# Layer 6: half 1's unrouted down products, the gate transposes and the bias products are issued behind the last routed tile

## What is computed

```python
xf = x.reshape(b * t, d)                     # 1024 tokens x 128
logits = xf @ Wg                             # 16 experts
_, topi = jax.lax.top_k(logits, 2)
gates = softmax(where(mask, logits, -inf))
y = 0
for e in range(16):                          # each token has 2 experts with a gate above 0
    h = silu(xf @ W1[e] + b1[e]) * (xf @ W11[e] + b11[e])        # 256 wide
    y = y + (h @ W2[e] + b2[e]) * gates[:, e, None]
z = silu(xf @ Ws1 + bs1) * (xf @ Ws11 + bs11) @ Ws2 + bs2        # 512 wide, every token
x = layernorm(x + y + z)
```

## Time and profile before

| | us |
|---|---|
| median of 3 runs | 660.75 |
| lowest, highest | 657.47, 665.46 |
| the profiled execution, its own time | 664.0 |
| its span in the profile | 662.2 |

### The profile page before, as it was taken

How to read it: one execution, slowest core, us unless ns; L and a number is a source line. 1 busy time by engine, 2 the same in 40 slices (tenths; PEclk the granted TensorE clock), 3 DMA queues, 4 the chain that set the end, 5 groups by cost and what they waited for, 6 DMA issues and landing times. The chain is left out here.

```text
span 662.2 us, 11995 instructions
## 1 busy us (share of the span) xinstructions
PE 469.6 (71%) x4136; PEld 363.4 (55%) x4136; DVE 442.6 (67%) x1480; ACT 266.9 (40%) x657; POOL 226.6 (34%) x265
## 2 busy tenths in 40 slices
PE   3788126583599768997858578968598895988850
PEld 2366113463577447775735457755377552687740
DVE  4899578979564776655583889974767572145535
ACT  5699511110013434653014637642375121165521
POOL 4131921636532002645010522310563136025540
PEclk9999657585799877997997768988899988899975
DMA  8100033100000040750000000000725001500112
GB/s 277 48 3 2 0 126 129 35 0 1 0 1 1 0 125 1 153 106 1 1 0 1 0 1 2 2 0 2 314 122 132 2 13 55 132 22 33 38 43 89
DMA packets 27966, 33.38 MB, mean 50 GB/s; under 512 B 4945, under 2 KB 21057, under 8 KB 27394
## 3 DMA queue, kind: packets, MB, share of 16 engines
q1 hardware_dynamic: 25970, 29.13, 14.9%
q0 software_dynamic: 1504, 3.15, 1.4%
q10 hardware_dynamic: 432, 0.33, 0.2%
HBM read 26.44 MB, written 6.16 MB: 49 GB/s over the span
## 5 line engine op out<-in xcount | busy, mean ns | idle before, releaser
L1789 POOL TENSOR_TENSOR ea_scaled_rows<-ea_scaled_rows 128x768 f32<-128x768 f32 (+2 forms) x24 | 27.8, 1156 | 62.0 <-ACT ea_scaled_rows L1716 60.8
L3210 POOL DMA_INDIRECT em_results<-em_y_slot,slot_rows x31 | 29.8, 960 | 51.5 <-DVE em_y_slot L3341 42.6
L3097 PE MATMUL banks<-em_slotT,em_weights 128*128 128x128 f32 x248 | 34.5, 283 | 4.2 <-ACT em_weights L2972 3.8
L219 ACT ACTIVATE norm_log<-norm_var 128x4 f32<-128x4 f32 x20 | 4.1, 205 | 82.2 <-DVE norm_var L197 82.1
L3332 DVE SCALAR_TENSOR_TENSOR em_innerT<-banks,em_bias_of,em_soft 128x128 f32<-128x128 f32 x62 | 18.8, 346 | 25.9 <-ACT em_soft L3156 23.5
L3097 PEld LDWEIGHTS banks<-em_slotT,em_weights 128*128 128x128 f32 x248 | 30.9, 196 | 6.1 <-issue 6.0
L1716 ACT ACTIVATE ea_scaled_rows<-banks,ea_gate 128x192 f32<-128x192 f32 x64 | 23.5, 419 | 26.0 <-PE banks L38 25.9
L3156 ACT ACTIVATE em_soft<-banks,em_bias_of 128x128 f32<-128x128 f32 x62 | 19.6, 374 | 27.2 <-remote 17.5
L2360 POOL TENSOR_TENSOR ga_to_end<-ga_cum 128x512 f32<-128x512 f32 x8 | 8.8, 1096 | 62.9 <-DVE ga_to_mid L2422 62.9
L3109 PE MATMUL banks<-em_down,em_innerT 128*128 x124 | 20.1, 289 | 6.8 <-DVE em_innerT L3332 6.8
L2747 POOL TENSOR_TENSOR ca_prob<-ca_prob,ca_most 128x1232 f32<-128x1232 f32 x8 | 18.0, 2249 | 17.6 <-DVE ca_most L2800 17.6
(11 more groups left out here) (505 smaller groups left out, 1527.0 us busy)
## 6 DMA issues: line engine op xcount, KB each, us to landing
em_up<-in_em_up SPq DMA_DIRECT2D x3, 1536.0 KB, 11.7
ea_wide<-ea_gates SPq DMA_DIRECT2D x4, 1024.0 KB, 16.4
em_down<-in_em_down SPq DMA_DIRECT2D x3, 768.0 KB, 13.1
em_slots<-slot_rows SPq DMA_DIRECT2D x1, 2108.0 KB, 11.2
w_qkv<-in_w_qkv SPq DMA_DIRECT2D x1, 1536.0 KB, 7.2
slot_rows<-em_slots SPq DMA_DIRECT2D x1, 1360.0 KB, 8.6
cos_lag<-in_cos_lag SPq DMA_DIRECT2D x1, 1024.0 KB, 5.6
sin_lag<-in_sin_lag SPq DMA_DIRECT2D x1, 1024.0 KB, 8.1
```

The lines of the kernel that those rows point to most:

```text
L1789: step(pool.tensor_tensor(scaled_rows[:, k, 0:n], scaled_rows[:, k, 0:n], scaled_rows[:, k, n:2 * n], ALU.add))
L3097: ins = pe.matmul(s.ps[:, k * P:(k + 1) * P], weights[:, n % NW, k // 2, k % 2 * P:(k % 2 + 1) * P], slotT[:, n], start=True, stop=True, s ...
L3210: pool.indirect_dma_start(core.results[:, :], bass.IndirectOffsetOnAxis(ap=slot_rows[:, s, P:P + 1].bitcast(U32), axis=0), y_slot[:, s % N ...
```

## The change

TensorE issues `bias_of` right behind the last `shared_up` product, then WARM, the transposes and the slots. `gateT`, `b2` and `shared_down(1)`, in this order, stand behind the last slot's down product. `plan` has the same order. ScalarE's two copies of `gateT` stand behind its part of the slots, ahead of the load of the table for Exp and Log. VectorE gathers `b2_0`, `b2_1` and `y_1` behind its part of the slots and waits until they are in `acc` before it goes on. `hidden` of pieces 2 and 3 stays where it is until then. No instruction is added or taken out besides waits, and no DMA is moved in any engine's program.

```diff
-        plan += ... up_banks(1) + ["y_0"] + up_banks(2) + up_banks(3) + ["y_1"]
-        plan += [f"gateT{b}" for b in range(B)] + [f"b2{b}" for b in range(B)] + ["bias_of"]
+        plan += ... up_banks(1) + ["y_0"] + up_banks(2) + up_banks(3) + ["bias_of"]
...
         for s in range(-1, SLOTS + 2):
             plan += [f"{k}{n}" for k, n in steps_of(s)]
+        plan += [f"gateT{b}" for b in range(B)] + [f"b2{b}" for b in range(B)] + ["y_1"]
...
     TensorE:
                 for n in (2, 3):
                     for j in range(2):
                         shared_up(n, j)
-                shared_down(1)
-                (gateT of both halves, b2 of both halves)
                 (bias_of, then turn, up and down of every slot, unchanged)
+                (gateT of both halves, b2 of both halves)
+                shared_down(1)
...
     ScalarE:
-                (the copies of gateT, behind the last Silu of the unrouted part)
...
                             stages[k](n)
+                for b in range(B):
+                    s = ring[f"gateT{b}"]
+                    s.ready(act)
+                    act.copy(gateT[:, half(b)], s.ps[0:NE, :]).then_inc(s.drained, 1)
                 load_exp_and_log(act)
...
     VectorE:
                 lift(2)
                 gather("y_0", 0)
                 lift(3)
-                gather("y_1", 1)
-                for b in range(B):
-                    ring[f"y_{b}"].taken(dve)
-                    gather(f"b2{b}", b)
...
                             stages[k](n)
+                ring["y_0"].taken(dve)
                 for b in range(B):
-                    ring[f"b2{b}"].taken(dve)
+                    gather(f"b2{b}", b)
+                ring["b21"].taken(dve)
+                gather("y_1", 1)
+                ring["b20"].taken(dve)
+                ring["y_1"].taken(dve)
                 dve.wait_ge(share_ready, 1)
                 dve.wait_ge(back_loaded[0], 16)
```

More of the change, by code:

```diff
@@ L2925, in expert_mlp @@
             plan += [f"xT{b}", f"logit{b}"]
-        plan += up_banks(0)[:2] + ["count"] + up_banks(0)[2:] + up_banks(1) + ["y_0"] + up_banks(2) + up_banks(3) + ["y_1"]
-        plan += [f"gateT{b}" for b in range(B)] + [f"b2{b}" for b in range(B)] + ["bias_of"]
+        plan += up_banks(0)[:2] + ["count"] + up_banks(0)[2:] + up_banks(1) + ["y_0"] + up_banks(2) + up_banks(3) + ["bias_of"]
         first_of = {lo: n for n, (lo, hi) in enumerate(GROUPS)}
@@ L3116, in _ @@
                         stages[k](n)
+                for b in range(B):
+                    s = ring[f"gateT{b}"]
+                    s.claim(pe)
+                    pe.wait_ge(gate_ready, 1)
+                    for i in range(HT):
+                        ins = pe.transpose(s.ps[0:NE, i * P:(i + 1) * P], gate[:, HT * b + i], ident[:, :])
+                    ins.then_inc(s.filled, 1)
+                for b in range(B):
+                    ring[f"gateT{b}"].taken(pe)
+                    s = ring[f"b2{b}"]
+                    s.claim(pe)
+                    for i in range(HT):
+                        ins = pe.matmul(s.ps[:, i * P:(i + 1) * P], gateT[:, HT * b + i], t["em_b2"][:, :],
+                                        start=True, stop=True, skip_group_check=True)
+                    ins.then_inc(s.filled, 1)
+                shared_down(1)
             @block.scalar
@@ L3137, in _ @@
                                        bias=b_gate[:, 2 * e + j:2 * e + j + 1]).then_inc(s.drained, 1)
[L3138 to L3141, removed]
                 def turn(n):
```

## The result

The changed kernel took 656.91 us (median of 20 runs, 648.57 to 662.22) against 661.88 us for the kernel before (20 runs, 657.47 to 665.53). The ratio is 0.9875, interval 0.9851 to 0.9899, some 8.3 us. It is formed over the runs within 1.5% of the fastest of their kernel, which are all 20 before but only 13 of the 20 after, so it leaves out the seven slowest on one side alone. The plain medians differ by 5.0 us, the means over all runs (662.04 and 655.71) by 6.3. So the change is faster here by 5 to 8 us, whichever is taken. The forecast was 9.9 us, 650.9.

What follows compares the result with a forecast made beforehand. TensorE's 16 us between VectorE's last `lift` and slot 0 were taken as the bound, slot 0's load as next limit. Terms -12.4 + 0 + 2.0 + 0 + 0.5 = -9.9 us; median 660.75 to 650.9, range 646.5 to 657.5.

Steps and rivals of the forecast that it cites:

- (a): Start of the slots: slot 0's transpose waits only for its load, at 565.0 instead of 577.4; gain 12.4 us.
- (b): Ahead of the first slot: bias copy at 561.0 to 561.8, weights by 564.2, later loads in time; cost nothing.
- (c): Start of the slots: TensorE idles, then runs at half clock for about 5 to 7 us; cost 2.0 us.
- Rival C: Slot loop: clock stays at half, up to 1.3 us a slot; chance 0.05 above 9 slots, 0.09 in mild form.
- (d): Slot loop: 31 slots take 61.9 us, nothing in it is edited, so it moves as a whole; 0 us.
- (e): End: the moved products behind the last down product are mostly hidden in 8.5 us before `y_back` is used; cost 0.5.
- rival A: End: `shared_down(1)` and what precedes it run at half clock, VectorE waits; 4.2 instead of 0.5 us; chance 0.12.
- all of it at half: End: case with all moved work at half clock, put at 13.9 us, late by 5.4.
- A shift of one stage carries over whole: Whole kernel: the 9.9 us gain applied unchanged from the profiled execution to the median, 660.75 to 650.9.
- B: Before the slots: TensorE itself late, WARM ends at 567.0, no clock cost; gain 9.8 us; chance within the forecast's 0.66.
- D: Slots' start or loop: bias completion held back, or scatters and late signals pace the loop; gain 0 to 4; chance 0.08.

Runs made afterwards that it cites:

- experiment 8: Changed kernel with WARM = 11: 640.97 us, 1.0001 to the kernel before; with `shared_down(1)` then five WARM products ahead of the slots: 644.13 us, 1.0026.

## Why the prediction was right, and where it wasn't

The direction was right for the executions that the prediction was made for. The size was forecast too large: 9.9 us, against 8.3 by the ratio, 6.3 by the means and 5.0 by the medians; 656.91 us lies inside the range, near its upper end. Its reason holds only there: where no signal is late, the same change is worth nothing (ratio 1.0003). And that the one profile after comes to 10.7 us, close to 9.9, is partly luck: the loop was 4.4 us shorter, which the prediction had at nothing, and the end 3.3 us longer than its term.

**(a) The start: right, under a condition that I took for fixed.** Forecast 12.4 us, measured 12.7. The rows were read rightly: the chain went through the moved work, and the load of slot 0 was the next limit. What the prediction doesn't say is what made it 12.4. `shared_down(1)` started 21.0 us behind S in that profile and 13.6 without late signals, 7.5 us; it took 6.15 instead of 3.81 us, because TensorE had been idle and stood at half clock, 2.3 us. Together 9.8 us of the 12.7 measured; some 2.8 are all that is left in the later profiles. So the change gains by taking a chain of three engines (product, Silu, `lift`, product) out from in front of the slots, a chain that late signals stretch. The unnamed waits of the earlier trace rows stood in the prediction, in (b), as a matter of when the bias copy can start; by this comparison of the same program with and without them, they are behind most of the gain at the start.

**(b) The bias and the weights: right.** The copy of the biases came 19.9 us behind S (556.82), where I had put it at 20.2 to 21.0, after an unnamed wait of 4.17 us; it was covered. (GpSimd's last scatter ended at 561.03, not at 561.8 as I had read from the window in the earlier trace rows; in both profiles the last late signal ahead of the slots comes within 0.3 us before that end.) ScalarE's timeline, with the copy of slot 0's transpose behind it:

```profile
556.82 0.26 ACT L3156 COPY em_bias_of<-banks 128x124 f32<-128x124 f32 x1 [4.17 <-remote]
...
561.34 0.27 ACT L3142 COPY em_slotT<-banks 128x128 f32<-128x128 f32 x1 [2.31 <-PE banks L3068]
```

**(c) The clock: right.** Forecast 2.0 us, measured 2.5; 0.50 for 10 us instead of 5 to 7. It appeared in every profile in which the slots wait for the load. The rule of the Trainium skill ("TensorE: Matmul & The Clock Gate", on the clock gate's oscillation), that pauses let the clock fall, agrees: an idle stretch of 3.7 us, and half clock for 10 us. The clock also fell where the pauses were shorter, 1.81 us and 1.31 us with only the transpose of 0.33 us between (experiment 8). Rival C, that it would stay for many slots, didn't happen; slot 3 was at full clock in each.

**(d) The loop: "moved as a whole" is the step that failed on a size I had at nothing.** It took 54.4 us before, 50.0 after, and 42.2 us with either kernel without late signals. So 12 us of the loop before, and 8 after, come with the late signals. My rows hinted at it: 52 records in 5.85 us make 1.35 us a slot of 12 records, while the loop took 61.9 us for 31 slots, 2.0 each, and I didn't ask where the rest went. The lateness isn't scattered: before, the unnamed waits of the Silu in the loop end at 594.07, 601.76, 609.48, 617.18, 624.89 and 632.58, one every 7.7 us, which is every four slots, and all but the first (2.2 us) last 3.0 to 3.1 us. After, they fall on other waits, of 0.8 to 1.8 us, up to 608 every 7.0 us, and one of 3.1 us comes at the end. So the two loops differ by a step that repeats. A further part is the clock: before, the loop's last slots ran at half clock for 3.3 us (635.1 to 638.4); after, the whole loop had full clock. Half of those 3.3 us, 1.7, is my estimate of what that cost at most. Whether the change makes the loop 4.4 us shorter or one execution differs from the next isn't settled, since no further profile had late signals. If the whole 4.4 were the change's, the steps would sum to 10.7; if none, to 6.3. The ratio's 8.3 lies between, the means' 6.3 at the lower end, the medians' 5.0 below both.

**(e) The end: the mis-sized term, by 3.3 us.** Forecast 0.5, measured 3.8, near rival A's 4.2. (Where I put "all of it at half" the sum is 14.1, not 13.9; nothing hung on it.) The sum took full clock for most of it, on the argument that TensorE is busy there after the change. It was; but an unnamed wait of 3.04 us ahead of the last down product (the first line of the chain above) had let it idle for 2.32 us, and the clock was 0.58 on the mean up to VectorE's next step. Without late signals the same products ran at full clock and were covered by 0.8 us, which is the cover that I had worked out (8.5 - 7.7).

**The sum against the median.** "A shift of one stage carries over whole" was too simple: the layers in front move S by up to 9 us from one execution to the next (537 to 546 in these profiles). The profiled execution after is the second fastest of 20, 7.5 us below its median, of which the early S can be about half (it came 3.9 us earlier than before). How large the steps of layer 6 were in the median execution, no profile shows.

**The rivals.** A came true in its mechanism in the profiled execution. B (TensorE itself late) fell: by it WARM would have been at work from 557 to 563, but slot 0's transpose, queued behind WARM, was done and copied by ScalarE at 561.34. D came true in the executions of the experiments only in its size (a gain of 0 to 4 us), by a mechanism that I hadn't named: there the slots were held by only 2.8 us to begin with.

## What to carry to other kernels

Before a stall is priced as a property of the program, look at who released it. Where the profile has no releaser for a wait for another engine of the same core, the time isn't explained by the program, and another execution may not have it: take a second profile of the unchanged kernel first. Fewer hand-overs between engines ahead of a critical step make it robust against that, and cost nothing here; but the time that a chain of work hides, and the clock that it keeps up, come back as a price when it is moved (2.5 of 2.8 us).

## What the runs showed of the hardware

- In the executions of the first comparison TensorE's completions reached the other engines up to several us after the products (39.0 us of unnamed waits before, 35.4 after; 6.0 us for the last `lift`), only in layer 6, where GpSimd issues its indirect scatters; ahead of the slots the last of them ended at 560.96, and GpSimd's 16 scatters at 561.03. In none of the 12 profiles of the experiments was there one, two of them of the kernel before and two of the changed kernel as they are. The difference is about 20 us of 661 for the kernel before, 16 of 657 for the changed one. I don't know its cause; whether it is the chip or something about the placement was not tried, and neither was the loop without scatters in its presence.
- TensorE at half clock ran slots 0 and 1's up products in 2.04 us against 1.13, and kept at work to within 1.81 us of the slots its clock still fell during slot 0. In the second profile of the kernel before, where products run up to the transpose with no gap over 0.23 us, the clock stayed at full through the first slots (7.5 us from the transpose to slot 3, against 10.0).
